# A Flamingo block on one core: who issues the first Q store and stack loads, and when the first batch's V pieces are made

## The reference

```python
x = x + tanh(g_xattn[0]) * xattn(layernorm(x), ctx, ctx, Wq, Wk, Wv, Wo)
x = x + tanh(g_ffn[0]) * ffn(layernorm(x), router_w, w1, w2)
...
# xattn
qh, kh, vh = (q @ Wq.T), (k @ Wk.T), (v @ Wv.T)      # split in 16 heads
attn = einsum('bhnc,bhlc->bhnl', qh * 256 ** -0.5, kh)
attn = softmax(attn, axis=2)                         # over the 512 tokens
attn = attn / sum(attn, axis=-1)                     # over the 1601 context rows
out = einsum('bhnl,bhlc->bhnc', attn, vh) @ Wo.T
```

## Time and profile before

| | us |
|---|---|
| median of 3 runs | 1813.04 (1812.7 to 1815.76) |
| the profiled execution | 1814.16 |
| its span in the trace | 1812.4 |
| PE busy | 1683.1 (93%) |
| DVE busy | 1419.2 (78%) |
| ACT busy | 1283.9 (71%) |
| POOL busy | 542.7 (30%) |

### The profile page before, as it was taken

One profiled execution on the slowest core, in us unless ns is written; L12 is line 12 of the kernel. 1 busy time (PEld: TensorE's weight loads), 2 busy tenths in 40 slices (PEclk: granted clock), 3 DMA queues, 4 the chain that ended last, 5 costly groups with the idle time before them and its releaser, 6 DMA issues.

```text
span 1812.4 us, 31594 instructions
## 1 busy us (share of the span) xinstructions
PE 1683.1 (93%) x9980; PEld 900.1 (50%) x9980; DVE 1419.2 (78%) x2293; ACT 1283.9 (71%) x3640; POOL 542.7 (30%) x825
## 2 busy tenths in 40 slices
PE   8989999999999989999999998887799999999997
PEld 5223233333333323333333332214799999999997
DVE  7979999999999999999999999997444444444442
ACT  5989999999999999999999999995111111111111
POOL 3331251352244225235223422213222222222222
PEclk9999999999999999999999999999899999999999
DMA  8547215613711731461272163419222222222221
GB/s 233 129 112 189 63 51 148 162 40 96 196 53 52 176 108 47 133 181 40 75 194 60 58 162 83 148 54 299 86 35 38 36 37 35 38 35 38 35 36 28
DMA packets 128245, 172.87 MB, mean 95 GB/s; under 512 B 14496, under 2 KB 105760, under 8 KB 128128
## 3 DMA queue, kind: packets, MB, share of 16 engines
q1 hardware_dynamic: 113152, 150.51, 30.3%
q0 software_dynamic: 14144, 20.44, 6.5%
q10 hardware_dynamic: 832, 0.53, 0.1%
HBM read 117.96 MB, written 53.47 MB: 95 GB/s over the span
## 4 chain that ended last, share of the span: by engine, by line
PE 36%; ACT 29%; DVE 20%; issue 7%; POOL 3%; DMA 3%; SPq 1%; POOLq 0%; DVEq 0%; ACTq 0%
ACT w_all L899 27%; DVE negmax L1080 14%; PE scores L1474 13%; PE scores L1487 13%; PE scores L716 3%; PE acc L729 3%; POOL routed_rows L1273 1%; DVE resid L975 1%; ACT w_all L857 1%; DMA out<-row_t,gate_token 1%; PE spare L579 1%; PE spare L573 1%; PE spare L1464 1%; DVE rz L1066 1%; SPq L389 1%
## 5 line engine op out<-in xcount | busy, mean ns | idle before, releaser
L899 ACT ACTIVATE w_all<-scores,negmax 128x512 f32<-128x512 f32 (+1 forms) x1664 | 1127.8, 751 | 24.8 <-DVE negmax L1080 19.3
L1080 DVE TENSOR_REDUCE negmax<-scores 128x2 f32<-128x1024 f32 (+1 forms) x832 | 1002.2, 1216 | 65.6 <-PE scores L716 59.2
L716 PE MATMUL scores<-q_stack,w_all 128*128 128x512 bf16 (+1 forms) x1664 | 501.9, 383 | 50.0 <-ACT w_all L899 48.3
L899 ACT ACTIVATION_READ_ACCUMULATOR w_all<-scores,negmax 128x1 f32 (+1 forms) x1664 | 449.3, 270 | 0.0
L729 PE MATMUL acc<-w_all,vz 128*32 128x512 f32 (+1 forms) x3328 | 443.7, 605 | 3.0 <-POOL vz L1296 2.8
L1515 ACT ACTIVATE projections<-scores 128x512 f32<-128x512 f32 x142 | 84.9, 598 | 449.0 <-PE scores L1474 449.0
L716 PEld LDWEIGHTS scores<-q_stack,w_all 128*128 128x128 bf16 (+1 forms) x1664 | 115.7, 99 | 524.9 <-ACT w_all L899 395.5
L1296 POOL TENSOR_TENSOR vz<-w_all,rz 128x68 f32<-128x68 f32 (+1 forms) x416 | 124.7, 300 | 789.3 <-DVE rz L1066 763.7
L1474 PEld LDWEIGHTS scores<-row_t,q_stack 128*128 128x128 f32 x2272 | 265.9, 193 | 7.6 <-issue 2.8
L1474 PE MATMUL scores<-row_t,q_stack 128*128 128x128 f32 x2272 | 267.5, 276 | 2.0 <-DVE row_t L1542 1.8
L1487 PE MATMUL scores<-room,projections 128*128 128x256 f32 x1136 | 256.8, 379 | 0.0
(11 more groups left out here) (208 smaller groups left out, 1027.8 us busy)
## 6 DMA issues: line engine op xcount, KB each, us to landing
w_all<-k_parts SPq DMA_DIRECT2D x248, 200.1 KB, 3.5
w_all<-in_w SPq DMA_DIRECT2D x16, 1024.0 KB, 10.8
q_stack<-q_parts SPq DMA_DIRECT2D x248, 64.0 KB, 3.4
k_parts<-parts SPq DMA_DIRECT2D x42, 300.0 KB, 2.9
w_all<-in_ctx_t SPq DMA_DIRECT2D x7, 1601.0 KB, 7.3
parts<-routed SPq DMA_DIRECT2D x71, 129.0 KB, 2.1
q_parts<-parts SPq DMA_DIRECT2D x14, 384.0 KB, 3.2
routed<-pad_row SPq DMA_DIRECT2D x8, 645.0 KB, 9.5
```

The costliest lines, as they stand in the source:

```text
L716: mm = pe.matmul(scores[0:r, 2 * (u % SLOTS) + j % 2, :], k_stacks[g][:, j, lt * P:lt * P + r], q_stack[:, g, j, :], start=True, stop=True)
L899: e = act.activation(probs[0:r, s % RING, j, :], scores[0:r, 2 * (u % SLOTS) + j % 2, :], ACT.Exp, bias=negmax[0:r, u % 4, j % 2:j % 2 + 1 ...
L1080: dve.tensor_reduce(negmax[0:r, u % 4, :], scores[0:r, 2 * (u % SLOTS):2 * (u % SLOTS) + 2, :], AX.X, ALU.max, negate=True).then_inc(negma ...
```

## The change

ACT issues the store of Q piece 0 (before its copy of K piece 4) and, once that has landed, the Q loads of blocks 0, 2, 4 and 6 (before its copy of K piece 7). POOL stores K piece 4, waits for the same store, and issues the other four loads. `EARLY` loses V pieces 1 and 2; they become whole (not halved) `own_v` fills in steps 0 and 1. The other `own_v` fills of batch 0 move to steps 3, 5, 7 and 8 (they were in 1, 3, 5 and 6), and every fill after them two steps later. PE waits in addition, in step 0's fill, for all early splits.

```diff
--- before.py
+++ after.py
@@ -80,26 +80,27 @@
 }
 LAST_BATCH_FILL_AT = {**FILL_AT, 44: ("tail", "pads", 0)}
 HALVED = ("k", "q", "v", "own_v", "out_proj")
-LAST_V = (("v", VF - 1), ("own_v", VF - 1))
+WHOLE = (("v", VF - 1), ("own_v", VF - 1), ("own_v", 1), ("own_v", 2))
 
 
 FIRST_BATCH_FILL_AT = {
-    1: ("cur", "own_v", 3), 3: ("cur", "own_v", 4), 5: ("cur", "own_v", 5), 6: ("cur", "own_v", 6),
-    11: ("next", "k", 0), 13: ("next", "k", 1), 15: ("next", "k", 2), 16: ("cur", "o_turn", 0),
-    18: ("next", "k", 3), 20: ("next", "k", 4), 22: ("next", "k", 5), 24: ("next", "k", 6), 26: ("next", "k", 7),
-    27: ("next", "x_turn", 0), 28: ("next", "x_turn", 1), 29: ("cur", "o_turn", 1), 31: ("next", "q", 0),
-    33: ("next", "q", 1), 35: ("next", "v", 0), 37: ("next", "v", 1), 39: ("next", "v", 2), 41: ("next", "v", 3),
-    42: ("cur", "o_turn", 2), 44: ("next", "v", 4), 46: ("next", "v", 5), 47: ("next", "v", 6),
-    48: ("cur", "attn_turn", 0),
+    0: ("cur", "own_v", 1), 1: ("cur", "own_v", 2), 3: ("cur", "own_v", 3), 5: ("cur", "own_v", 4), 7: ("cur", "own_v", 5),
+    8: ("cur", "own_v", 6), 13: ("next", "k", 0), 15: ("next", "k", 1), 17: ("next", "k", 2), 18: ("cur", "o_turn", 0),
+    20: ("next", "k", 3), 22: ("next", "k", 4), 24: ("next", "k", 5), 26: ("next", "k", 6), 28: ("next", "k", 7),
+    29: ("next", "x_turn", 0), 30: ("next", "x_turn", 1), 31: ("cur", "o_turn", 1), 33: ("next", "q", 0),
+    35: ("next", "q", 1), 37: ("next", "v", 0), 39: ("next", "v", 1), 41: ("next", "v", 2), 43: ("next", "v", 3),
+    44: ("cur", "o_turn", 2), 46: ("next", "v", 4), 48: ("next", "v", 5), 49: ("next", "v", 6),
+    50: ("cur", "attn_turn", 0),
 }
 
 
 EARLY = (("k", 0), ("k", 1), ("x_turn", 0), ("x_turn", 1), ("k", 2), ("q", 0), ("k", 3), ("k", 4), ("k", 5), ("k", 6),
-         ("k", 7), ("q", 1), ("v", 0), ("v", 1), ("v", 2))
+         ("k", 7), ("q", 1), ("v", 0))
 EARLY_SPLIT = [piece for piece in EARLY if piece[0] in ("k", "q")]
 EARLY_COPIED = [piece for piece in EARLY if piece[0] not in ("k", "q")]
 BANKS_EARLY = 8
 WARM_TURNS = 24
+Q_BLOCKS_OF_ACT = (0, 2, 4, 6)
 WARM_PROJECTED, WARM_ROUTING, WARM_ROWS = 12, 20, 20
 ORDER = [KC + i for i in range(KC * KCHUNK)] + list(range(KC))
 LOGITS = 22
@@ -136,10 +137,10 @@
     def halves(self, s):
 
         now, after = self.fill(s), self.fill(s + 1)
-        begun = after and after[0] in HALVED and after not in LAST_V
+        begun = after and after[0] in HALVED and after not in WHOLE
         assert not (begun and now) or now[0] in HALVED
         if now:
-            split = now[0] in HALVED and now not in LAST_V
+            split = now[0] in HALVED and now not in WHOLE
             return [(now, (1,) if split else (0, 1))]
         return [(after, (0,))] if begun else []
 
@@ -327,7 +328,7 @@
     fill_taken = sem("fill_taken")
     early_ctx = [sem(f"early_ctx_{c}") for c in range(KCHUNK)]
     early_k_in = [sem(f"early_k_in_{half}") for half in range(2)]
-    early_q_in = sem("early_q_in")
+    early_q_in = [sem(f"early_q_in_by_{queue}") for queue in ("act", "pool")]
     early_ready = sem("early_ready")
     early_split = sem("early_split")
     early_copied = sem("early_copied")
@@ -647,6 +648,7 @@
                 if (name, i) == ("own_v", len(EARLY_COPIED) - KC) and 0 in halves:
 
                     pe.wait_ge(early_copied, len(EARLY_COPIED))
+                    pe.wait_ge(early_split, len(EARLY_SPLIT))
                 mm = project_v(spare, i, halves)
             elif name == "o_turn":
 
@@ -698,7 +700,8 @@
 
                 wait(pe, stack_in[g], stacks_by(b + 1, g))
                 if b == 0 and g == 0:
-                    pe.wait_ge(early_q_in, 16 * BLOCKS)
+                    pe.wait_ge(early_q_in[0], 16 * len(Q_BLOCKS_OF_ACT))
+                    pe.wait_ge(early_q_in[1], 16 * (BLOCKS - len(Q_BLOCKS_OF_ACT)))
                     pe.wait_ge(early_k_in[0], 16 * BLOCKS)
             if b == 0 and g == 0 and p == 0 and lt == HALFWAY // P:
                 pe.wait_ge(early_k_in[1], 16 * BLOCKS)
@@ -706,7 +709,7 @@
             wait(pe, exp_done, b * UNITS + (u - SLOTS + 1 if u >= SLOTS else (-1, 0, -2)[u]))
             if b == 0 and u < SLOTS:
 
-                held = EARLY[u * 2 + 1 + BANKS_EARLY]
+                held = EARLY[min(u * 2 + 1 + BANKS_EARLY, len(EARLY) - 1)]
                 if held in EARLY_SPLIT:
                     pe.wait_ge(early_split, EARLY_SPLIT.index(held) + 1)
                 else:
@@ -821,6 +824,12 @@
             act.wait_ge(dve_setup, DVE_SETUP)
             act.activation(tgx[:, :], zero[:, :], ACT.Tanh).then_inc(tanh_ready, 1)
             for n, (name, i) in enumerate(EARLY):
+                if (name, i) == ("k", 4):
+                    store_early(act, "q", 0)
+                if (name, i) == ("k", 7):
+                    stored_early(act, ("q", 0))
+                    for blk in Q_BLOCKS_OF_ACT:
+                        load_q_block(act, early_q_in[0], 0, 0, blk)
                 act.wait_ge(early_ready, n + 1)
                 bank = early_bank(n)
                 if name in ("q", "k"):
@@ -1276,11 +1285,12 @@
 
             pool.wait_ge(mv_ready, NT)
             one_over_deviation(mv1, rstd1, rstd_step, 0)
-            store_early(pool, "q", 0)
+            store_early(pool, "k", KCHUNK)
             stored_early(pool, ("q", 0))
             for blk in range(BLOCKS):
-                load_q_block(pool, early_q_in, 0, 0, blk)
-            for i in range(KCHUNK, 2 * KCHUNK):
+                if blk not in Q_BLOCKS_OF_ACT:
+                    load_q_block(pool, early_q_in[1], 0, 0, blk)
+            for i in range(KCHUNK + 1, 2 * KCHUNK):
                 store_early(pool, "k", i)
             store_early(pool, "q", 1)
             pool.dma_start(out[TOKENS:TOKENS + P, :], pad_row[:, 0:D]).then_inc(rows_out, 16)
```

## The result

The changed kernel took 1816.42 us, the median of 15 runs (1811.34 to 1820.06), against 1813.56 for the kernel before, of 15 runs beside it. The ratio is 1.0015 [1.0008, 1.0022]: 2.9 us more, less than the 0.2% of the prediction's bound, but above its range, and on the other side of it. Its profiled execution took 1814.89 (1814.16 before), its span is 1813.0.

A forecast was written before the change was run, and what follows sets the result against it. ACT's exponentials were taken to bound attention. Start -0.8, gap before K piece 6 -0.8, shifted fills +0.2 and border 0 sum to -1.4: 1812.8 against the profiled 1814.16, 1811.6 against the median 1813.04; range 1809.8 to 1815.0.

The forecast's parts named there:

- the prediction's bound: Whole kernel: a measurement can tell about 0.2%, 3.6 us, from no change.
- the start's term: Start of batch 0: second pair of exponentials at 30.95 against 32.26, then one V copy, -0.8; bounds -1.3 and +0.8.
- The gate: Start: the first scores' weight load, waiting for the Q stack, opens at 26.4 instead of 28.3.
- up to all of the 1.9: Start: busy DMA engines may stretch the Q landing, at most by the whole 1.9 gained before the first scores.
- the first rival: Start: Q stack lands no earlier, DMAs sharing busy engines; +0.8 in place of -0.8, time 1813.2, no change; chance 0.17.
- Its "against": Start, argument against the Q stack landing no earlier: issue, not bytes, paces the loads.
- V behind the gate: Start: V piece 1 follows the first scores, 27.2 to 29.1; its ACT copy precedes the first exponential at 29.6.
- ACT and DVE: Start: ACT's Q loads delay DVE's last split to 28.0 from 26.93, leaving 1.25 of the 1.9 gained.
- The gap before K piece 6: Middle of batch 0: ACT's idle 4.68 moves to step 26 and shrinks to 3.9, -0.8; bounds 0 and -0.8.
- +0.2: Shifted fills: DVE's K piece 7 beside its `acc` copy, attention transpose ending nearer the border; bounds 0 and +0.5.
- the V copy's +0.5: Start: one more ACT copy of a V piece to pay by the end of step 8, about 0.5.
- The border: Border to batch 1: context load lands at 185.8, 0.5 ahead of PE's 186.31, costing 0; at a landing of 8.8, +1.8.

The follow-up runs named there:

- e2: Changed kernel with 24 idle transposes on PE between V piece 0 and the first scores; 1817.43 us, ratio to before 1.0012.
- h2: Kernel before with ACT's Q store and half the Q loads, K piece 4's store first, and group 3 loads behind all eight K stores; 1810.01 us, 0.9967.
- g3: Kernel before with SP's 16 group 3 stack loads of batch 0 behind all eight K stores; 1808.32 us, ratio 0.9961.
- e1: The changed kernel itself again, as baseline of a group on another chip; 1815.49 us, ratio to before 0.9999.
- f1: The changed kernel unaltered, another single profiled execution; 1818.69 us.
- f2: The changed kernel unaltered, a further single profiled execution; 1814.46 us.
- h1: Changed kernel with SP's group 3 loads behind six K stores, so without the gap before K piece 6; 1809.95 us, ratio to before 0.9971.
- e4: Kernel before with only the V pieces and fill table moved as in the change, POOL issuing all of Q; 1817.26 us, ratio 1.0011.
- e6: Changed kernel with POOL's store of K piece 4 behind its Q loads again; 1814.68 us, ratio to before 1.0008.
- g2: Changed kernel with K piece 4's store behind POOL's Q loads and 20 idle PE transposes; 1817.33 us, ratio to before 1.0009.
- g1: Changed kernel with 36 idle transposes on PE between V piece 0 and the first scores; 1816.84 us, ratio to before 1.001.
- g4: Kernel before with ACT issuing only the Q store, V piece 2 alone a fill, table shifted, group 3 loads behind six K stores; 1807.75 us, 0.9955.
- e7: Kernel before with only batch 0's fill table shifted by two steps; 1815.69 us, ratio to before 1.001.
- e3: Kernel before with only ACT's Q store and half the Q loads, POOL storing K piece 4 first; 1815.64 us, ratio 1.0003.
- e5: The kernel before, unaltered, profiled anew; 1812.96 us, ratio to before 0.9996.
- f3: Kernel before with only the fill table shifted by two steps, another single profiled execution; 1814.90 us.
- e8: Kernel before with ACT issuing only the Q store, POOL all Q loads, V piece 2 alone a fill, table shifted; 1812.67 us, ratio 0.9998.

## Why the prediction was wrong, step by step

**The step that failed is the start's term: -0.8 forecast, with mark 1 at 30.95.** It came at 34.76, 3.8 later than forecast, in two parts that add up. The gate, forecast at 26.4, opened at 28.80: 2.4. V piece 1, forecast at 1.89, took 3.26: 1.4. From the first exponential to the second pair it took 1.34 against the 1.35 forecast. (0.2 of the gate's 2.4 is where the span starts: counted from Q piece 0's split the forecast had mark 1 at 13.3, and the four traces of the changed kernel have 16.5 to 17.1.)

*The gate.* The issues came as worked out: store 17.84 (forecast 17.7), landed by 21.3 (21.6), POOL's last load issued at 24.1 (23.7). I had put the landing at the median of before, 2.7, and named the stretch "up to all of the 1.9" as a bound only. In the eleven traces with loads from ACT and POOL together the medians were 4.0 to 5.3, in the nine with POOL alone 2.4 to 3.4. The gate opened at 27.8 to 29.9 (30.4 in e2) with both, and at 27.8 to 29.3 with POOL alone. That is the first rival, which I gave 0.17, and its mechanism, the shared and busy DMA engines, fits their share of 1.08 against 0.73. Its "against" (issue, not bytes, paces the loads) was wrong: once issue is quicker, the landing is what paces them. The Trainium skill ("DMA: Bandwidth & Descriptors", "Issuing engines are not separate DMA queues") has issue from more engines save only the sequencer's time. By that rule the split can gain no more than that time; h2 against g3 (marks 0.3 later) gained none of it.

*The clock.* It stood nowhere in the prediction. I took V piece 1 at the 1.89 of a busy PE, though I moved it, and piece 2 with it, out of the time that kept PE busy ahead of the gate. With those 3.8 us of matmuls gone PE idles for 3.3 to 4.1, and in four traces of five (after, e1, f1, f2; not h1) the clock fell. It fell too in e2 and not in e4 and e6. With V piece 1 or both still early it fell in no trace ahead of the first exponentials.

*V behind the gate.* This part was priced, and rightly: with the clock full, h1, e4, e6 and g2 go from gate to mark 1 in 4.27 us (g1 in 4.4), the forecast in 4.55. The kernel before needs 3.87, g4, where half a V piece follows the first scores but ACT waits for no copy, 3.40. So with the gate unmoved this part loses 0.4 even at the full clock.

*ACT and DVE.* DVE's last split ended at 28.93, forecast 28.0; 0.5 of the 0.9 is that ACT came back at 24.70 and not at 24.2. DVE then idled for 0.96, so it was not the last. Had the stack landed at 26.4, DVE would have been: two maxima of 1.23 from 28.93 end at 31.4, mark 1 would stand at about 31.5 with the clock at full speed, and 0.8 of the 1.3 forecast would be left (an estimate).

**The gap before K piece 6: right in size.** 3.9 forecast, 3.40, 3.58, 3.50 and 3.84 in the four traces. Piece 3's way from ACT's copy to its last part took 5.4 (5.6 forecast). Not foreseen: the lower clock behind it. From mark 1 to mark 2 the four traces of the changed kernel took 292.7 to 294.5, the two of before 294.3 and 294.7: 0.6 less on average, where -0.1 was forecast (-0.8, +0.2 and the V copy's +0.5). No run tells the +0.2 by itself. **The border: right**, 0. *The range:* its lower end, 1809.8, doesn't follow from the working, which gives 1810.9 less 0.3, 1810.6; the miss lies at the other end.

**Together:** at mark 2 the mean of the four traces is 328.7 (327.4 to 329.7), of the two of before 327.0 (326.6 and 327.5). So the start's 2.3 and the middle's -0.6 make the change some 1.7 us slower by so few traces; the medians say 2.9 on one chip and 0.3 on the other.

**Open:** whether loads issued by two engines land later by themselves or for the K stores that POOL then sends sooner (K piece 4's store explains a part in e6, and not in g2); which executions lose the clock after the same idle time; and why the medians of e4, e6 and e7 are 1.2 to 2.2 above before while their marks aren't, so how much of the changed kernel's 2.9 is the shifted table's.

## What to carry to other kernels

Before work is moved from ahead of a wait to behind it, price the engine that now waits: here PE's clock fell ahead of the first exponentials in some of the traces without that work and in none with it, and the work lay in the way when the wait ended. When a wait rests on issue and on landing, a quicker issue is only worth what the landing leaves, so move the issue alone first, as e3 did. And when two kernels differ by less than their runs do, compare marks inside the traces, from an event that neither changes; the largest gain here, 7.0 us, was in a row that the prediction took as given, 16 loads ahead of a store in an in-order queue.

## What was not expected of the hardware

The granted clock fell to 1.2 GHz behind a PE idle for 2.50 us (e2) and not behind one of 4.09 (h1) or 3.00 (e4). Where it fell, up to mark 2, it stayed down for 3.4, 6.8 or 10.2 us and nothing between; behind the gap the same kernel shows 3.4 (before, after) and 6.8 (e5, e1), and the shifted one 6.8 and 10.2 (e7, f3). The same 64 KB block loads landed in 2.1/2.6/3.1 us issued by POOL (e8), with the DMA engines' share at 0.73, and in 4.9/5.3/5.8 by ACT and POOL (h1), at 1.08.
